# An embedding gather in front of a pairwise-interaction tower: another schedule of gathers, additions and transposes

## The reference

```
e = stack([tbl_f[ids[:, f]] for f in range(40)], axis=1)    # 512 x 40 x 64
vi, vj = e[:, i_idx, :], e[:, j_idx, :]                     # all pairs i < j: 780
z = einsum('bpe,bpe->bp', einsum('bpd,pde->bpe', vi, W), vj)
h = concatenate([z, dense_ctx], axis=1)                     # 512 x 796
h = relu(h @ W_top1 + b_top1)                               # 512
h = relu(h @ W_top2 + b_top2)                               # 256
y = h @ W_top3
```

## Time and profile before

| | |
|---|---|
| median of 3 executions | 319.71 us (319.37 to 320.14) |
| the profiled execution: span | 361.1 us |
| time that the profiled execution took outside its span | none is given; the span is its own time here |
| PE busy | 324.8 us (90%) |
| DVE busy | 255.2 us (71%) |
| POOL busy | 206.5 us (57%) |
| ACT busy | 106.8 us (30%) |
| mean granted TensorE clock | 0.957 of full |

### The profile page before, as it was taken

The page is one execution under the profiler, slowest core; times in us unless marked ns, Lnnn a source line. Parts: engine busy times, 40 slices in busy tenths (PEclk is TensorE's granted clock), DMA queues, the critical chain, the costliest instruction groups (busy, mean ns, idle before and its releaser), DMA issues.

```text
span 361.1 us, 4423 instructions
## 1 busy us (share of the span) xinstructions
PE 324.8 (90%) x1700; PEld 115.7 (32%) x1700; DVE 255.2 (71%) x249; ACT 106.8 (30%) x266; POOL 206.5 (57%) x178
## 2 busy tenths in 40 slices
PE   7999739699888949949959999989999999999997
PEld 2444213133222313312312333333333333333455
DVE  5996535586676856945847899999999999990000
ACT  0216000060505551350767653025049000001032
POOL 3887737354735625634654538989987677770000
PEclk9999988899989969987998999999999999999999
DMA  7941212112212272302211346867798766650000
GB/s 170 337 154 51 60 32 66 43 47 73 57 42 53 78 257 92 79 21 52 73 51 42 81 86 147 176 145 158 151 193 172 170 136 118 117 109 9 15 0 0
DMA packets 17772, 35.34 MB, mean 98 GB/s; under 512 B 3924, under 2 KB 4952, under 8 KB 17624
## 3 DMA queue, kind: packets, MB, share of 16 engines
q0 software_dynamic: 7408, 16.26, 23.4%
q1 hardware_dynamic: 7848, 13.96, 12.9%
q10 hardware_dynamic: 2496, 4.84, 3.9%
HBM read 22.86 MB, written 0.00 MB: 63 GB/s over the span
## 4 chain that ended last, share of the span: by engine, by line
PE 59%; DVE 19%; issue 8%; POOL 6%; another core or an unknown queue 6%; DMA 1%; ACT 0%; DVEq 0%; POOLq 0%
PE y_ps L664 33%; PE z_ps L687 15%; DVE prod L558 14%; PE y_ps L697 4%; POOL prod L378 3%; POOL gathered L349 2%; DVE prod L484 2%; PE t_ps L697 2%; PE y_ps L743 1%; PE t_ps L571 1%; POOL prod L374 1%; DMA lane_rows_sb<-lane_rows 1%; DVE zT L494 1%; DVE x_quad L490 1%
## 5 line engine op out<-in xcount | busy, mean ns | idle before, releaser
L664 PE MATMUL y_ps<-x,w 64*128 64x512 f32 x780 | 190.0, 619 | 29.6 <-DVE prod L558 21.9
L349 POOL DMA_INDIRECT gathered<-in_tbl,ids_sb x128 | 131.2, 1025 | 94.6 <-DVE prod L558 55.9
L558 DVE TENSOR_TENSOR prod<-y_ps,x 128x1024 f32<-128x1024 f32 x89 | 103.8, 1216 | 54.8 <-PE y_ps L664 27.5
L664 PEld LDWEIGHTS y_ps<-x,w 64*128 64x128 f32 x780 | 70.6, 189 | 146.6 <-issue 104.0
L558 DVE TENSOR_TENSOR prod<-y_ps,x_quad 128x1024 f32<-128x1024 f32 x96 | 110.6, 1215 | 3.8 <-PE y_ps L664 1.9
L687 PE MATMUL z_ps<-prod,select 128*32 128x512 f32 x596 | 81.7, 652 | 1.2 <-POOL prod L378 1.2
L417 ACT COPY x<-x_fold 32x128 f32<-32x128 f32 x176 | 52.0, 295 | 84.2 <-DVE x_fold L527 70.6
L378 POOL TENSOR_TENSOR prod<-prod 128x1024 f32<-128x1024 f32 x23 | 55.3, 2406 | 0.8
L374 POOL DMA_DIRECT2D prod<-prod x23 | 21.6, 939 | 22.4 <-DVE prod L558 16.3
L687 PEld LDWEIGHTS z_ps<-prod,select 128*32 128x32 f32 x596 | 15.3, 114 | 59.4 <-issue 39.5
L440 ACT COPY x_mix<-x 64x512 f32<-64x512 f32 x40 | 24.7, 616 | 0.7
(11 more groups left out here) (47 smaller groups left out, 84.8 us busy)
## 6 DMA issues: line engine op xcount, KB each, us to landing
w<-w_rows SPq DMA_DIRECT2D x48, 256.0 KB
prod<-prod POOLq DMA_DIRECT2D x23, 512.0 KB, 4.6
gathered<-in_tbl,ids_sb POOLq DMA_INDIRECT x128
w<-w_rows ACTq DMA_DIRECT2D x1, 1792.0 KB
prod<-in_tbl ACTq DMA_DIRECT2D x6, 256.0 KB
prod<-hot_ids SPq DMA_DIRECT2D x4, 256.0 KB, 3.9
prod<-in_tbl ACTq DMA_DIRECT2D x4, 128.0 KB, 3.3
w<-w_rows ACTq DMA_DIRECT2D x1, 512.0 KB
```

The costliest lines, as they stand in the source:

```text
L349: nc.gpsimd.indirect_dma_start(gathered[:, slot, c, s * DIM:(s + 1) * DIM], None, tables[f][:, :], bass.IndirectOffsetOnAxis(ap=ids_sb[:, ...
L558: nc.vector.tensor_tensor(prod[:, d % PROD_SLOTS, :, :], y_ps[:, d % DUO_SLOTS, :, :], factor, ALU.mult).then_inc(prod_ready, 1)
L664: last = nc.tensor.matmul(y_ps[:, d % DUO_SLOTS, half, :], w[rows, r % W_SLOTS, d % ROUND, :], x[rows, units[half], :], start=True, stop=True)
```

## The change

Only constants change; the functions stay as they are.

- Units 9, 10 and 11 leave `FOLDED`: PE transposes them (12 transposes and 3 one-instruction ACT copies in place of 3 DVE folds and 48 small ACT copies). They are then due before duos 38, 46 and 56 on PE, not before duos 33, 41 and 49 on DVE. Units 12, 13 and 14 become the ones folded inside a round (before duos 57, 65 and 73; before the change 60, 68 and 76).
- 30 gathers are free, not 16; then three are listed for each of rounds 0 to 13, four for rounds 14 to 19 and one for rounds 20 to 23; 28, not 16, are listed for rounds 24 to 34. Unit 16 is folded before duo 104 (round 26; before the change 92), unit 17 before duo 116 (round 29; 100), unit 18 before duo 132 (round 33; 124), unit 19 before duo 144 (round 36; 144).
- Six quad rounds are summed unadded, 24, 26, 27, 29, 31 and 33, not only round 29.

```diff
--- before.py
+++ after.py
@@ -38,14 +38,14 @@
 GATHER_LEAD = 2
 FOLD_LEAD = 6
 
-FOLDED = range(9, 20)
+FOLDED = range(12, 20)
 INSIDE = 3
 
-GATHERED_FIRST = 16
-
-ROUND_GATHERS = [4] * 24
-LATE_GATHERS = [1, 1, 2, 1, 1, 3, 1, 2, 1, 2, 1]
-UNADDED = [29]
+GATHERED_FIRST = 30
+
+ROUND_GATHERS = [3] * 14 + [4] * 6 + [1] * 4
+LATE_GATHERS = [4, 1, 4, 3, 1, 4, 1, 4, 1, 4, 1]
+UNADDED = [24, 26, 27, 29, 31, 33]
 
 
 def pair_index(i, j):
```

## The result

The changed kernel takes 327.81 us (median of 4 executions, 325.42 to 328.66), the kernel before 319.54 (median of 4, 319.13 to 320.14). The ratio is 1.0242, 95% interval 1.0202 to 1.0282: slower by 8.3 us, where 5.8 were forecast and the range ended at 328.8. The profiled execution of the changed kernel took 328.66 us, 1.9 us more than its span of 326.8.

What follows compares the result with a forecast made beforehand. PE was taken to set the pace before the quads and to be level with DVE in them. Terms 1.95 + 4.3 - 1.2 + 0.7 = +5.75 us on 319.7 gave 325.5 us, range 320.8 to 328.8.

Steps and rivals of the forecast that it cites:

- The reading of the stalls: Rounds 2 to 23: timed runs hardly have the profiled stalls, excess 41.0 us, and go at PE's pace.
- The close match of 41.0 and 41.4 us: Excess of rounds 2 to 23 over PE's pace, 41.0 us, against profiled execution minus other runs' median, 41.4 us.
- units 9 to 11 by PE: Three units transposed in rounds where PE sets the pace, 0.65 us each: +1.95 us, bounds 0 and +1.95.
- five more unadded sums, less the wait on POOL: Quad rounds 24, 26, 27, 31, 33: 0.86 us more PE each, +4.3; round 28's addition wait goes, -1.2 us.
- wait on the z copy: Round 33: ACT handles unit 18 and saves block 3 before PE's sum of round 32: +0.7 us, bounds 0 and 1.0.
- freed gathers: Gathers 16 to 29 lose a gate that was already open: worth 0.
- four gathers inside an addition: Additions of rounds 25, 28, 30, 32 still in time, by 1.1 and 0.2 us: 0, bounds 0 and +1.3.
- nothing waits for a gather that comes too late: Rounds 2 to 23 at PE's pace: gathers land in time, unit 7's by 57.9, due at 60.0.
- A lag of POOL on the old chain: Rival: POOL reaches round 24 late in timed runs, so the change is faster; 317.5 us at L = 8; chance 7%.
- Early gather waits: Rival: old folds wait for late gathers, PE's later transposes don't; faster, 317 to 319 us; chance 5%.
- nothing moves: Rival: PE's added 6.25 us finds idle time; 319.7 to 320.3 us; chance 4%.
- The worse case: Rival: late additions of rounds 25, 28, 30 and 32 each cost 1 us or more; 329 to 331 us; chance 7%.

Runs made afterwards that it cites:

- The second profile of before: The kernel before, unchanged, profiled again: span 320.2 us for an execution of 322.07 us.
- the better list: Kernel before with four late gathers moved into rounds 12, 15, 18 and 21, folds of units 17 and 18 earlier, nothing unadded: 317.57 us, ratio 0.9941.
- the two experiments on single parts: Kernel before with only units 9 to 11 transposed by PE, 321.62 us; kernel before with only rounds 24, 26, 27, 29, 31, 33 unadded, 323.78 us.
- the transposes alone: Kernel before with FOLDED = range(12, 20) alone, so PE transposes units 9, 10 and 11: 321.62 us, ratio 1.0049.
- another kernel: The changed kernel with UNADDED = [29] as before, its late gathers kept: 331.99 us, ratio 1.0388.

## Why the prediction was right, point by point

*The reading of the stalls* held, and the forecast hangs on it. The second profile of before and the changed kernel's profile have no such stalls, and rounds run at 5.49 us. The close match of 41.0 and 41.4 us was luck: a span was set against times that are 1.9 us longer than their spans, and span against span (361.1 and the 317.7 of a timed execution of 319.49 us) the profile is 43.4 us longer. The stalls had also cost 2.6 us before round 2, where the count began, and 41.0 + 2.6 is that 43.4 to 0.2.

*The steady terms.* Lowest execution against lowest, the changed kernel is 6.3 us slower (325.42 against 319.10). Stages without a wait, put together from several profiles, show 5.9 of it:

| term | forecast | measured |
|---|---|---|
| units 9 to 11 by PE | +1.95 | +2.17 (134.77 - 132.60) |
| five more unadded sums, less the wait on POOL | +4.3 - 1.2 | +3.04 (118.36 - 115.32) |
| wait on the z copy | +0.7 | +0.35 |
| the first product of round 24 | not foreseen | +0.36 |
| freed gathers | 0 | 0 |
| four gathers inside an addition | 0 | 0, no wait on POOL |
| sum | +5.75 | +5.92 |

The whole quad stage is 3.75 us longer (119.07 - 115.32); 0.34 of that is the border that moves with the transposes and comes back behind it. That the sum is met to 0.2 us is in part luck: +0.22 and +0.36 stand against -0.35.

The z copy term was mis-sized on PE's side: block 3 is saved at 224.62, 9.85 us after the round's start at 214.77, against +9.95 forecast, but PE asks only at 224.33, +9.56, where I had +9.1 to +9.3. The duos of round 33 take 4.08 us instead of 3.70, since DVE's fold of unit 18 at 215.85 holds up the products that free their banks. No run was made for that cause, but the profiles bear it out: in the quad rounds duos of 4.07 or 4.08 us stand only in rounds with a fold, 36 before (224.16), 33 in the changed kernel, 29 and 36 with the better list (186.89, 219.67). The last has one more of them than before, which fits its gain of 1.75 us in place of 2.06. The transposes were sized by their row; the pace of the rounds, 6.28 against 5.49, is the right price.

*What the forecast lacked* is the difference between the steady 5.9 and the median's 8.3 us: 2.4 us. In the profiled execution the wait for unit 7 and the lower clock behind it cost 3.6 us (138.71 against 135.13); what the three others waited for was not seen, though two of them have its mean clock, 0.995. The step that failed is the sentence that nothing waits for a gather that comes too late. I set the times of the unstalled rounds by round 2's first product at 42.49, from a profile that had already lost time; without stalls it begins at 39.6 to 40.6. So unit 7 is due at 57.1, not at 60.0. Its last gather starts at 54.26, not at 53.3, and takes 4.8 us until PE can start, where I had 4.6 as the most. The room that I counted was not there. That the median still lies within the range is luck: no term of the sum or of its upper bound stands for this wait.

*Rivals.* A lag of POOL on the old chain did not show, and the quad stage of before repeats to 0.03 us. Early gather waits did come, but for unit 7, which PE transposes in both kernels, and no fold of before waited for its gathers, so nothing was given back. That nothing moves falls with the two experiments on single parts, +2.17 and +3.04 us. The worse case, late additions at 329 to 331, did not come: PE waited for no addition, with 1.06 us to spare in round 25 and 0.27 in round 30 (forecast 1.1 and 0.2).

**What stays open.** Of the changed kernel's 10 executions 8 lie more than 1 us above the lowest; of before's 39 on the later chips 10 do. Two waits that can be behind it are seen in profiled executions: unit 7's last gather (in both kernels) and the first small table's second half (in the changed kernel, and with the old `UNADDED` and gather lists in the transposes alone). Behind the first product the stages of one kernel repeat to 0.1 us between its two profiles, but for the waits on gathers. How late unit 7 is depends on the head as well: in the profiles POOL's gather 16 starts at 33.05 to 37.11 us, as one or two of the gathers before it take 3 to 5 us. Neither freeing the gathers nor moving POOL by +1.25 or -2.5 us brought or removed the spread, and the kernel with the old lists has it too. Why it comes more often in the changed kernel was not found. On the chip that ran both, it is 5 of 6 executions against 2 of 10; were the two kernels alike in this, so uneven a split would come about once in 40 times. Chance is unlikely, but not excluded.

## What to carry to other kernels

Compare a profiled execution with the timed ones, span with span, before you price a wait in it: here 43 us of waits were in the one and not in the others, and stages that repeat (a round's pace, start to start) gave every term to within 0.4 us. Where one engine is full, price a moved step by how much longer its round becomes, not by its own row. When gathers and additions share one queue, first ask where in the kernel that queue has room: four gathers moved into rounds 12, 15, 18 and 21, of rounds that have 0.49 us to spare each, gave back both an addition's wait and an unadded sum (both edits were made in one run, not apart).

## What the runs showed of the hardware that was not expected

- The span of one profiled execution was 361.1 us and that of another, of the same kernel, 320.2. In the first, DVE waited up to 5.83 us and began its products at 130.51, though the trace has the matmuls that they need starting from 123.78 on and done by 126.6.
- A wait of 1.87 us on PE was followed by the lower clock (12 instructions in 4.16 us, not 2.85), while one of 1.57 us was not (the same 12 in 2.85), and one of 2.28 us in another kernel was not either (16 in 3.70). So the length of a wait alone does not tell what follows. Taken together the 1.87 us cost 3.6 us.
- A gather took POOL 0.94 us in most of the kernel, and 4.83 to 5.13 us once or twice in the head of 11 of the 12 profiles. Which gather it is differs between executions of one kernel: the eighth in the first profile of before (15.88), the sixth in the second (15.66).
- The span is 1.9 us shorter than the time of the same execution (326.8 and 328.66, 315.7 and 317.57).
